# A graph layer with experts on one core: the first sort's places ahead of the table of products, zeros read from the cleared sums, a longer pipeline in the nodes stage

## What is computed

```
xn  = layernorm(x)                                        # per node
agg = segment_sum(xn[dst], src);  cnt = edges per node
gnn = xn @ W1.T + b1 + (agg / max(cnt, 1)) @ W2.T + b2
k, v = head-wise layernorm(xn) * weights + biases         # 8 heads of 32
mix = xn @ blockdiag(k.T @ v / N) + xn
x1  = x + gnn + mix
h   = layernorm(x1);  logits = h @ gate_w + gate_b        # 8 experts
e, prob = argmax, softmax(logits)[argmax];  pos = running count of e
y   = (relu(h @ w1[e] + b1[e]) @ w2[e] + b2[e]) * prob    # if pos < 977
out = x1 + y
```

## Time and profile before

| | us |
|---|---|
| median of 3 runs | 2044.88 |
| lowest, highest | 2043.13, 2045.44 |
| profiled execution, its own time | 2044.0 |
| its span | 2042.3 |
| PE busy, share of the span | 1529.3 (75%) |
| DVE busy | 1362.1 (67%) |
| POOL busy | 985.9 (48%) |
| ACT busy | 724.3 (35%) |
| mean granted TensorE clock | 0.816 of 2.4 GHz |

### The profile page before, as it was taken

How to read it: one execution, slowest core, us unless ns; L and a number is a source line. 1 busy time by engine, 2 the same in 40 slices (tenths; PEclk the granted TensorE clock), 3 DMA queues, 4 the chain that set the end, 5 groups by cost and what they waited for, 6 DMA issues and landing times. The chain is left out here.

```text
span 2042.3 us, 27345 instructions
## 1 busy us (share of the span) xinstructions
PE 1529.3 (75%) x6558; PEld 883.5 (43%) x6558; DVE 1362.1 (67%) x3717; ACT 724.3 (35%) x1992; POOL 985.9 (48%) x970
## 2 busy tenths in 40 slices
PE   4659997567877777365655558788673999999997
PEld 3434432233333333133332335445463666666665
DVE  6679998789999988466666557656672244444444
ACT  5349994005878777000000002111362222222221
POOL 0000103777777777777777777777154011111111
PEclk9779998678999999555555558787555999999999
DMA  5110071333333333843333334444354222223300
GB/s 155 42 42 22 24 318 47 99 102 100 97 99 99 96 96 99 89 117 100 101 98 98 97 110 134 124 130 131 125 185 140 94 95 94 101 93 101 101 9 5
DMA packets 86860, 204.49 MB, mean 100 GB/s; under 512 B 19874, under 2 KB 49096, under 8 KB 83728
## 3 DMA queue, kind: packets, MB, share of 16 engines
q0 software_dynamic: 49488, 131.52, 23.2%
q1 hardware_dynamic: 28524, 64.16, 9.0%
q10 hardware_dynamic: 8700, 7.07, 1.2%
HBM read 157.43 MB, written 49.89 MB: 102 GB/s over the span
## 5 line engine op out<-in xcount | busy, mean ns | idle before, releaser
L512 POOL DMA_INDIRECT w<-xn_parts,idx x830 | 854.4, 1029 | 289.0 <-issue 236.3
L1049 DVE TENSOR_TENSOR XA<-XA,bank 128x257 f32 x878 | 367.0, 418 | 282.1 <-PE bank L789 253.1
L788 PE MATMUL bank<-w,S 128*128 (+1 forms) x878 | 292.9, 336 | 280.6 <-SPq L460 134.9
L788 PEld LDWEIGHTS bank<-w,S 128*128 128x128 f16 x878 | 92.6, 105 | 488.8 <-issue 312.6
L789 PE MATMUL bank<-w,S 128*128 (+1 forms) x878 | 297.8, 342 | 0.0
L1818 POOL DMA_INDIRECT out<-ob,tok x64 | 66.5, 1039 | 402.0 <-DVE ob L1804 385.6
L610 ACT ACTIVATE LV<-LH,v 125x128 f16<-125x128 f16 x600 | 182.1, 387 | 191.2 <-DVE LH L1299 191.0
L1742 PE MATMUL bank<-w,ht 128*117 128x256 f32 (+1 forms) x1024 | 223.7, 379 | 0.0
L1731 PE MATMUL bank<-xt,w 128*128 128x468 f32 (+1 forms) x512 | 215.7, 580 | 0.8 <-ACT xt L1756 0.8
L1766 ACT ACTIVATE ht<-bank,b1c 128x468 f32<-128x468 f32 (+1 forms) x128 | 85.7, 669 | 334.2 <-PE bank L1731 334.2
L1742 PEld LDWEIGHTS bank<-w,ht 128*117 128x117 f32 (+1 forms) x1024 | 188.8, 186 | 30.5 <-issue 0.4
(11 more groups left out here) (291 smaller groups left out, 2291.6 us busy)
## 6 DMA issues: line engine op xcount, KB each, us to landing
w<-f SPq DMA_DIRECT2D x16, 1024.0 KB, 7.6
expert_rows<-w SPq DMA_DIRECT2D x7, 2048.0 KB, 20.3
w<-xn_parts,idx POOLq DMA_INDIRECT x830, 2.8
xb<-expert_rows SPq DMA_DIRECT2D x8, 1028.0 KB, 11.1
xb<-expert_rows SPq DMA_DIRECT2D x8, 939.7 KB
XA<-x SPq DMA_DIRECT2D x6, 1024.0 KB, 5.6
xn_parts<-w POOLq DMA_DIRECT2D x12, 512.0 KB, 3.5
work<-x ACTq DMA_DIRECT2D x48, 128.0 KB, 2.1
```

What stands on the lines that cost most here:

```text
L512: pool.indirect_dma_start(ring[:, o:o + 2 * D], None, tab, bass.IndirectOffsetOnAxis(ap=idx[:, t:t + 1], axis=0)).then_inc(s_g[t % RING], 16)
L788: pe.matmul(psA[t % AR][:, 0:AGW], lhs, ring_high[:, ds(o, AGW)], start=True, stop=True)
L1049: v.tensor_tensor(XA[:, ds(o, AGW)], XA[:, ds(o, AGW)], psA[t % AR][:, 0:AGW], ALU.add).then_inc(s_ev, 1)
```

## The change

Four things change.

- **Order in stage 1.** All products of the table move into the first sort (`late_at(g) = 1 + 10 * g // 3`, 25 groups over 84 of the 88 blocks of columns). Masks, counts and ranks of the first chunk follow each other; between them, at fixed masks and ranks, stand the layer norm statistics (`pair_stats`) and, some masks or ranks later, the scales (`pair_scale`). The rank matmuls rotate over four PSUM banks instead of two, and the norms of W2 go to another bank (`psQ`).
- **Columns by values.** Every fourth column instead of every fifth.
- **Zeros.** `expert_rows` is filled from the cleared sums in XA, in three DMAs that SP issues after the loads of x. POOL no longer clears `G` and no longer waits for the fill; DVE waits for it before its first add.
- **Distances in the nodes stage.** The reciprocal comes three steps after the standard deviation, the transpose two steps after the normal, the exponential and the prefixes three steps after what they read, and routing is spread over eight steps of unequal size, a later part before an earlier one of the next batch. `nrs` and `nmr` are doubled.

```diff
 LN_EPS, HEAD_EPS = 1e-5, 1e-5
+ZROWS = NX * CAPR * RW // (P * AGW)
+assert ZROWS * P * AGW == NX * CAPR * RW
...
 CHUNKS = chunk_plan()
-VEVERY = 5
+VEVERY = 4
...
-RB0, RB1 = 2, 4
+RB0, RB1 = 4, 4
 REST = 3
...
 PAIRS = NB // (2 * LD)
-RANKS = (16, 17, 16)
-EARLY = len(RANKS) + 1
 GROUPS = 4 * PAIRS + 1
-assert sum(RANKS) == NB and EARLY < PAIRS and COLS0 % LB == 0
+assert COLS0 % LB == 0 and NB == 8 * PAIRS + 1
...
-    return 3 + 5 * (g - 4 * EARLY)
+    return 1 + 10 * g // 3
...
-        sp.wait_ge(s_zero, 1)
-        flat, zeros = buf.rearrange("r w -> (r w)").rearrange("(p n) -> p n", p=P), G[:, 0:GR * 2 * D].bitcast(F32)
-        per, width = NX * CAPR * RW // P, GR * D
-        for o in range(0, per, width):
-            sp.dma_start(flat[:, o:min(o + width, per)], zeros[:, 0:min(width, per - o)]).then_inc(zst, 16)
+        sp.wait_ge(s_agg, 1)
+        flat = buf.rearrange("r w -> (r w)").rearrange("(p n) -> p n", p=P)
+        for o in range(0, ZROWS, NB):
+            n = min(NB, ZROWS - o)
+            sp.dma_start(flat[:, o * AGW:(o + n) * AGW].rearrange("p (b w) -> p b w", w=AGW),
+                         XA[:, 0:n * RW].rearrange("p (b w) -> p b w", w=RW)[:, :, 0:AGW]).then_inc(zst, 16)
         sp.wait_ge(s_dec, 2)
...
         pool.wait_ge(s_tb[1], 16 * n)
-        pool.memset(G[:, 0:GR * 2 * D].bitcast(F32), 0.0).then_inc(s_zero, 1)
         pool.memset(G2[:, 2 * D:GR * GW:GW], 1.0).then_inc(s_one, 1)
-        pool.wait_ge(zst, 16 * -(-(NX * CAPR * RW // P) // (GR * D)))
         pool.memset(G[:, 2 * D:GR * GW:GW], 1.0).then_inc(s_one, 1)
...
-        def table_of(i):
-
-            for g in range(4 * i, 4 * i + 4):
-                turned(g, 2)
-                if g == 0:
-                    act.wait_ge(s_parts, 1)
-                if g > 4 * i:
-                    high(g - 1, 2)
-            high(4 * i + 3, 2)
-
         normals(0)
...
         act.activation(parts[:, 1:2], parts[:, 1:2], ACT.Sqrt).then_inc(s_w2r, 1)
-        for i in range(1, EARLY):
-            normals(i)
-            table_of(i - 1)
-        for i in range(EARLY, PAIRS):
+        for i in range(1, PAIRS):
             normals(i)
...
         normal(0, 1, NB - 1, 2 * PAIRS + 1)
-        table_of(EARLY - 1)
+        act.wait_ge(s_parts, 1)
...
         for col in range(COLS0):
-            for g in range(4 * EARLY, GROUPS):
+            for g in range(GROUPS):
                 if col == LB * (late_at(g) + 1):
...
             ins.then_inc(s_tm, 1)
-
-        def table_of(i, between):
-
-            turn(4 * i, 8 * i, 2)
-            for g in range(4 * i, 4 * i + 4):
-                between(g % 4)
-                if g < 4 * i + 3:
-                    turn(g + 1, 2 * g + 2, 2)
-                table(g, 2)
-            between(4)
...
         for k in range(2):
-            ins = pe.matmul(psP[:, 0:D], ones[:, :], w2s[:, k * D:(k + 1) * D], start=(k == 0), stop=(k == 1))
+            ins = pe.matmul(psQ[:, 0:D], ones[:, :], w2s[:, k * D:(k + 1) * D], start=(k == 0), stop=(k == 1))
         ins.then_inc(s_w2n, 1)
-        def first_chunk(i, part):
-
-            if i == 0:
-                for b in range(NB * part // 5, NB * (part + 1) // 5):
-                    counted(0, b, psP)
-                if part == 4:
-                    place(psQ)
-            else:
-                b0, n = sum(RANKS[:i - 1]), RANKS[i - 1]
-                for b in range(b0 + n * part // 5, b0 + n * (part + 1) // 5):
-                    ranked(0, b, (psP, psQ))
-        for i in range(EARLY):
-            table_of(i, lambda part: first_chunk(i, part))
+        for b in range(NB):
+            counted(0, b, psP)
+        place(psQ)
+        for b in range(NB):
+            ranked(0, b, (psP, psQ, psV[0], psV[1]))
         pe.wait_ge(s_cp, NB)
...
         for col in range(COLS0):
-            for g in range(4 * EARLY, GROUPS):
+            for g in range(GROUPS):
                 nb = 1 if g == GROUPS - 1 else 2
...
-        def lows(i):
-
-            for h in range(2):
-                low(h, LD, i * 4 + 2 * h + 1)
-
-        def pair(i, back=None):
+        def pair_stats(i):
...
                 stats(h, LD, lambda j: xcols(i * (2 * LD) + (h * LD + j)))
-            if back is not None:
-                lows(back)
+
+        def pair_scale(i):
+
             if i:
...
-        def last():
+        def last_stats():
             v.wait_ge(s_xl, 16)
             stats(0, 1, lambda j: xcols(NB - 1))
+
+        def last_scale():
             v.wait_ge(s_xn, 2 * n)
...
         v.tensor_tensor(w2s, W2[:, :], W2[:, :], ALU.mult).then_inc(s_w2s, 1)
-        pair(0)
-        v.wait_ge(s_w2n, 1)
-        v.tensor_reduce(parts[:, 1:2], psP[:, 0:D], AX.X, ALU.max).then_inc(s_w2m, 1)
-        v.wait_ge(s_w2r, 1)
-        step(v.tensor_scalar(parts[:, 1:2], parts[:, 1:2], TINY, 1.0 / PARTS, ALU.max, ALU.mult))
-        wait()
-        v.reciprocal(parts[:, 0:1], parts[:, 1:2]).then_inc(s_parts, 1)
+
+        def largest():
+            v.wait_ge(s_w2n, 1)
+            v.tensor_reduce(parts[:, 1:2], psQ[:, 0:D], AX.X, ALU.max).then_inc(s_w2m, 1)
+
+        def parts_scale():
+            v.wait_ge(s_w2r, 1)
+            step(v.tensor_scalar(parts[:, 1:2], parts[:, 1:2], TINY, 1.0 / PARTS, ALU.max, ALU.mult))
+            wait()
+            v.reciprocal(parts[:, 0:1], parts[:, 1:2]).then_inc(s_parts, 1)
...
-        pair(1)
+        after_mask = {16: lambda: pair_stats(0), 24: lambda: pair_scale(0), 28: largest,
+                      36: lambda: pair_stats(1), 44: lambda: pair_scale(1)}
         for b in range(NB):
             mask_of(0, b, b)
-        v.wait_ge(s_parts, 1)
+            if b in after_mask:
+                after_mask[b]()
+        parts_scale()
         step(v.memset(mcoli[:, :], 0))
+        wait()
         place(psP, psQ)
-        for j, many in enumerate(RANKS):
-            pair(j + 2, j)
-            if j + 1 == len(RANKS):
-                for i in range(EARLY + 1, PAIRS):
-                    pair(i)
-                last()
-            for r in range(sum(RANKS[:j]), sum(RANKS[:j + 1])):
-                rank(0, r, (psP, psQ))
-        for r in range(NB, NB + RB0):
-            rank(0, r, (psP, psQ))
+        after_rank = {2: lambda: pair_stats(2), 9: lambda: pair_scale(2), 14: lambda: pair_stats(3), 21: lambda: pair_scale(3),
+                      26: lambda: pair_stats(4), 33: lambda: pair_scale(4), 38: lambda: pair_stats(5),
+                      45: lambda: pair_scale(5), 48: last_stats, 51: last_scale}
+        for r in range(NB + RB0):
+            rank(0, r, (psP, psQ, psV[0], psV[1]))
+            if r in after_rank:
+                after_rank[r]()
         v.wait_ge(s_cp, NB)
...
         step(v.tensor_copy(lane16[0:EP, 0:COLS0], tli[0:EP, 0:COLS0]))
-        lows(EARLY - 1)
         wait()
...
             tiles = CHUNKS[0][3]
-            for u in range(2 * EARLY, 2 * PAIRS + 1):
+            for u in range(2 * PAIRS + 1):
                 if k == LB * (late_at(min(2 * u + 1, GROUPS - 1)) + 5):
...
         v.wait_ge(s_agg, 1)
+        v.wait_ge(zst, 16 * -(-ZROWS // NB))
         for t in range(T0):
...
     nsd = sb("nsd", [P, NQ], F32)
-    nrs = sb("nrs", [P, NQ], F32)
-    nmr = sb("nmr", [P, NQ], F32)
+    nrs = sb("nrs", [P, 2 * NQ], F32)
+    nmr = sb("nmr", [P, 2 * NQ], F32)
     ut = sb("ut", [P, 2 * D], F32)
...
     NT = NB // NQ
-    NORM, GATE = NQ + 1, NQ + 2
+    STD, RECIP, NORM, GATE = NQ + 1, NQ + 4, NQ + 5, NQ + 7
     ROUTE = GATE + NQ + 1
-    STEPS = (NT - 1) * NQ + ROUTE + NQ
+    EXP, PREFIX = ROUTE + 3, ROUTE + 3
+    PARTS_OF_ROUTE = ((0, 1, 2), (3, 4, 5), (6,), (), (9, 10, 11), (12, 13, 14), (15, 16, 17), (7, 8, 18, 19))
+    STEPS = (NT - 1) * NQ + ROUTE + len(PARTS_OF_ROUTE)
...
         for n in range(STEPS):
-            t = batch(n, NORM)
+            t = batch(n, STD)
             if t is not None:
                 act.wait_ge(s_nv, t + 1)
+                if t:
+                    act.wait_ge(s_nr, t)
                 act.activation(nsd[:, :], nmv[:, 1:2 * NQ:2], ACT.Sqrt, bias=eps[:, :]).then_inc(s_ns, 1)
...
                     act.wait_ge(s_nr, m // NQ + 1)
-                act.activation(XA[:, m * RW:m * RW + D], XA[:, xcols(m)], ACT.Identity, bias=nmr[:, m % NQ:m % NQ + 1],
-                               scale=nrs[:, m % NQ:m % NQ + 1]).then_inc(s_x2, 1)
-            t = batch(n, ROUTE + 1)
+                o = m % (2 * NQ)
+                act.activation(XA[:, m * RW:m * RW + D], XA[:, xcols(m)], ACT.Identity, bias=nmr[:, o:o + 1],
+                               scale=nrs[:, o:o + 1]).then_inc(s_x2, 1)
+            t = batch(n, EXP)
             if t is not None:
...
                 ins.then_inc(s_u, 1)
-            t = batch(n, ROUTE + 3)
+            t = batch(n, PREFIX)
             if t is not None:
...
         for n in range(STEPS):
-            t = batch(n, NORM)
+            t = batch(n, RECIP)
             if t is not None:
                 v.wait_ge(s_ns, t + 1)
```

(19 more changed lines are left out.)

2 lines of the change are left out of this document (1 added, 1 removed).

## The result

The changed kernel took 1998.78 us (median of 4 runs, 1996.27 to 2003.29), the kernel before 2045.16 us (2043.13 to 2046.42) beside it: ratio 0.9777, 95% interval 0.9757 to 0.9796. The forecast was 1989 (1973 to 2007), faster: the sign and the range held, and the gain was 46 us where 55 were forecast. The profiled execution took 1998.75 us, its span is 1997.1, which is 45.2 us less than before.

What follows compares the result with a forecast made beforehand. Stages run in sequence, with gathers (1107 us) and experts (467 us) untouched. Saving 37.9 us at the first gather (-52.4 places, +14.5 sort) and 16.9 in nodes, 54.8 in all, gives 1989 us, range 1973 to 2007.

Steps and rivals of the forecast that it cites:

- Places first: Stage before the first sort: DVE loses waits and low halves, first lane one-hot at 95.5 us, 52.4 us sooner.
- The new wait of the masks: Before the sort: counting matmuls queue on PE behind products of `w2s`, early masks run at PE's pace, 0.5 us.
- The table inside the sort: First sort: 16 more product groups there, 192 us taken between 182 and 201, 14.5 us longer than 177.5.
- PE's term: First sort: PE's work on column blocks and table groups, 88 x 1.33 + 24.5 x 2.16 = 170 us.
- First gather: End of the first sort: first gather moves from 332.9 to 295.0 us, 37.9 us saved.
- Zero fill: Fill of `expert_rows`: already hidden, so dropping POOL's wait saves nothing; some 87 us from about 40 us on.
- Nodes: Nodes stage: longer distances bring a scatter batch from 13.6 to 10.9 us, 16.9 us saved (13 to 21).
- Gathers and experts: Gather and expert stages: untouched by the edit, 1107 and 467 us as before.
- The sort pays more for its groups: Rival, first sort: 2.0 us a group, sort 214 us, 22 more than taken, total 2011; chance 0.09.
- the others: Remaining rivals: sort at fullest engine 0.10, nodes tied 0.09, function change 0.02, zero fill/stores 0.03, slower 0.02, no effect 0.01.

Runs made afterwards that it cites:

- experiment 6: Changed kernel with two PSUM banks instead of four for the ranks' prefix matmuls: 2004.07 us, ratio 0.9792 (chip A).
- experiment 1: Changed kernel with ACT's high halves four blocks after the transposes instead of three, DVE's low halves six instead of five: 2152.63 us, ratio 0.9742 (chip B).
- Experiment 4: Changed kernel with the old zero fill (POOL clears half the ring after the last store, SP writes, POOL waits): 2206.58 us, ratio 0.9989 (chip B).
- experiment 9: Changed kernel, table groups a block earlier, each hand-over except the product on its transposed copy one block longer: 2165.25 us, ratio 0.9726 (chip C).
- experiment 10: Changed kernel with the high and low halves one block later, run again on chip C: 2168.14 us, ratio 0.9746.

## Why the prediction was right, and where it was off

- **Places first: right.** 52.4 us forecast, 54.5 measured. DVE's idle time fell by 41.9 us (42.1 - 0.5 forecast) and its busy time by 12.6 (10.8 forecast, the low halves; the other 1.8 were not foreseen). The new wait of the masks is 1.0 us, not 0.5. That the waits of the earlier trace rows would go since no products stand between the rank matmuls is shown by experiment 6.
- **The table inside the sort: the term that was mis-sized.** The prediction had ACT pay 1.47 us a group, "0.33 of it waiting for the group's product on PE", and added a little for rings, 192 us in all. The pace was ACT's, as said, but the wait is 0.91 us in each group: 24.5 x 0.58 = 14 us over the 190.4 us that ACT has with the old wait, 204 in all. This is beyond the 201 us at which the prediction said it would fall in this term. The wait of the earlier trace rows was read as a price of a group; it is a price of the place where `high` stands, one block behind the products, and that block had changed: with `VEVERY = 4` ACT makes six copies in it instead of eight, and 2 x 0.2925 is the 0.58 us by which the wait grew. The 0.2925 us stood in the prediction's own sums. That the place sets the wait is shown by experiment 1. PE's term of this part was low as well: 170 us, where PE is busy 193.9 in the window. The same formula gives 88 x 1.33 + 8.5 x 2.16 = 135 us for the kernel before, in which the earlier trace rows has 166.4. It did not decide the outcome, since in experiment 1 the same work of PE ends 16 us sooner.
- **First gather.** 295.0 forecast, 305.07 measured: +12.1 of the sort, -2.0 of the places.
- **Zero fill: right for the sum, wrong in what was said of it.** That "dropping POOL's wait saves nothing" holds for the kernel before; the prediction did not price the old fill behind a table whose last store lands at 297 us. Experiment 4 shows that the move is what makes the rest worth anything: 37.0 us at the first gather. Its landing at about 130 us, by the loads of x, held.
- **Nodes: right, with some luck.** Cadence 10.9 against 10.9, fourth batch within 0.2 us, last scatter 16.6 us sooner relative to the first gather against 16.9. Two small errors hide in this. The earlier trace rows has 20 waits, 17 without the three longest, not 18; with 17 the pace comes out at 10.7. And from the last gather, the stage is 18.3 us shorter, while the gathers in front of it took 1.7 us longer, start to start. As for ACT, the nine table loads stand with 1283 ns each and 0.1 us in all before either group of them, as in the earlier trace rows, and ACT is busy 9.50 and 8.90 us of two batches of 10.96 and 10.93 us, each with two loads. The Trainium skill ("ScalarE: Activation LUTs", What ACT_TABLE_LOAD costs) adds a drain of 1.38 us to each switch; by that figure ACT would need some 12.3 and 11.7 us for these batches, an estimate. They took 10.96 and 10.93, so here, too, the trace does not agree with it.
- **Gathers and experts: right**, 1108.0 and 466.1 us against 1107.1 and 466.9.
- **Rivals.** *The sort pays more for its groups* (2011) came true in its price (2.06 us a group, on ACT), not in its mechanism, a PE without idle time that DVE waits for: with the high halves a block later the sort with the same work takes 16 us less, and DVE's waits for PE at the lane one-hots fall from 15.8 us to 5.5. None of the others is seen in the trace.

The best kernels measured are the one with the halves a block later and `VEVERY = 5` on chip A (0.9694, 16.8 us below the changed kernel there) and the one of experiment 9 on chip C (0.9726, 2.9 us below experiment 10, the intervals of the two ratios overlap). The two steps together did not run.

## What to carry to other kernels

A wait in a row is the price of a place in an order, not of the work behind it: before multiplying it by more of that work, ask how far the waiting instruction stands behind its releaser in the new order, and whether that distance can be made one unit longer for nothing. When work is moved later, look for what starts only after it has ended: here a fill that had been free would have taken back the whole gain. In a software pipeline try each distance alone; here one of them held most of the gain. Mark such a comparison from the last event in front of the stage, since what lies before it varies from run to run by more than a step is worth.
